# The order of small reductions on VectorE in a two-layer convolution kernel

## What is computed

```python
def _gn(v, G=8, eps=1e-5):
    g = v.reshape(B_, H_, W_, G, C_ // G)
    m = jnp.mean(g, axis=(1, 2, 4), keepdims=True)
    s = jnp.var(g, axis=(1, 2, 4), keepdims=True)
    return ((g - m) / jnp.sqrt(s + eps)).reshape(v.shape)

kern = jnp.einsum('lj,lk,li->ijkl', u, w, v)      # 3 x 3 x 16 x 16
y = lax.conv_general_dilated(_gn(x), kern, padding='SAME', ...)
x = x + jax.nn.relu(y + b)
```

## Time and profile before

| | |
|---|---|
| median of 3 runs | 5166.48 us (5156.98 to 5170.72) |
| profiled execution, device time | 5165.69 us |
| its span, first to last instruction | 5163.9 us |
| TensorE matmuls busy | 4731.3 us (92%) |
| VectorE busy | 2715.9 us (53%) |
| ScalarE busy | 2198.9 us (43%) |
| GpSimd busy | 1261.3 us (24%) |
| mean busy share of the DMA engines | about 0.3, 108 GB/s |
| chain of work that ended last | TensorE 88%, "issue" 9% |
| mean granted TensorE clock | 0.967 of full speed |

### The profile page before, as it was taken

One profiled execution on the slowest core, in us unless ns is written; L12 is line 12 of the kernel. 1 busy time (PEld: TensorE's weight loads), 2 busy tenths in 40 slices (PEclk: granted clock), 3 DMA queues, 4 the chain that ended last, 5 costly groups with the idle time before them and its releaser, 6 DMA issues.

```text
span 5163.9 us, 291702 instructions
## 1 busy us (share of the span) xinstructions
PE 4731.3 (92%) x139776; PEld 2677.6 (52%) x139776; DVE 2715.9 (53%) x3148; ACT 2198.9 (43%) x2242; POOL 1261.3 (24%) x1093
## 2 busy tenths in 40 slices
PE   6999999999999999999999999999999999999999
PEld 3555555555554555555555555555554555555555
DVE  4555555555555555555555555555555555555554
ACT  4343443444434434444344443443434434434343
POOL 3231222322212223122232231222312222222120
PEclk9999999999999999999999999999999999999999
DMA  3333333333333333333333333333333333333322
GB/s 113 102 108 109 105 113 106 112 109 106 113 106 105 113 106 109 109 110 109 106 112 109 110 108 109 102 116 104 110 105 110 111 104 112 109 102 117 103 84 97
DMA packets 542288, 555.89 MB, mean 108 GB/s; under 512 B 16432, under 2 KB 541104, under 8 KB 541104
## 3 DMA queue, kind: packets, MB, share of 16 engines
q1 hardware_dynamic: 541104, 537.22, 31.8%
HBM read 268.72 MB, written 268.44 MB: 104 GB/s over the span
## 4 chain that ended last, share of the span: by engine, by line
PE 88%; issue 9%; ACT 0%; DVE 0%; ACTq 0%; DVEq 0%
PE ps_y L379 35%; PE ps_y L337 26%; PE ps_x L404 11%; PE ps_x L359 9%; PE ps_y L341 4%; PE ps_y L311 2%; PE ps_x L292 1%; PE ps_x L302 0%; ACT relu L459 0%; PE ps_y L317 0%; ACT relu L462 0%; DVE result L564 0%; DVE pixels L579 0%; ACTq L457 0%; DVEq L95 0%
## 5 line engine op out<-in xcount | busy, mean ns | idle before, releaser
L379 PE MATMUL ps_y<-odds,scaled 32*32 32x512 f32 x49152 | 1876.0, 645 | 3.8 <-issue 0.5
L337 PE MATMUL ps_y<-evens,scaled 32*32 32x512 f32 x46080 | 1741.9, 598 | 11.6 <-issue 2.4
L379 PEld LDWEIGHTS ps_y<-odds,scaled 32*32 32x32 f32 x49152 | 879.0, 106 | 820.2 <-issue 414.8
L564 DVE TENSOR_TENSOR result<-ps_x,relu 128x2048 f32<-128x2048 f32 x256 | 586.7, 2292 | 1170.1 <-PE ps_x L404 920.7
L567 DVE TENSOR_TENSOR odds<-ps_x,relu 128x2048 f32<-128x2048 f32 x256 | 586.8, 2292 | 1125.7 <-PE ps_x L359 874.2
L462 ACT ACTIVATE relu<-ps_y,bias 128x2048 f32<-128x2048 f32 x256 | 503.7, 1968 | 1567.4 <-PE ps_y L379 1416.0
L337 PEld LDWEIGHTS ps_y<-evens,scaled 32*32 32x32 f32 x46080 | 816.7, 103 | 608.0 <-issue 185.5
L273 POOL TENSOR_TENSOR fold<-fold,evens 128x1024 f32<-128x1024 f32 x384 | 844.2, 2198 | 567.3 <-DVE evens L551 490.3
L459 ACT ACTIVATE relu<-ps_y,bias 128x2048 f32<-128x2048 f32 x256 | 503.6, 1967 | 932.4 <-PE ps_y L311 493.7
L404 PE MATMUL ps_x<-odds,constants 32*32 32x512 f32 x16384 | 776.7, 606 | 0.0
L359 PE MATMUL ps_x<-evens,constants 32*32 32x512 f32 x16384 | 767.9, 596 | 0.0
(11 more groups left out here) (46 smaller groups left out, 1513.3 us busy)
## 6 DMA issues: line engine op xcount, KB each, us to landing
out<-pixels SPq DMA_DIRECT2D x512, 512.0 KB, 3.5
raw<-in_x SPq DMA_DIRECT2D x256, 512.0 KB, 3.9
raw<-in_x SPq DMA_DIRECT2D x128, 576.0 KB, 4.2
raw<-in_x SPq DMA_DIRECT2D x128, 448.0 KB, 3.5
parameters<-in_params SPq DMA_DIRECT2D x2, 96.5 KB, 2.0
constants<-in_consts SPq DMA_DIRECT2D x1, 81.0 KB, 2.1
```

The costliest lines, as they stand in the source:

```text
L337: done = nc.tensor.matmul(ps_y[part, r, :], w0[rows, t * Q:(t + 1) * Q], N0[rows, k:k + EACH, i:i + HQ], start=(t == 0), stop=(t == NTAP - 1))
L379: done = nc.tensor.matmul(ps_y[Q * r:Q * (r + 1), q, :], w1[p % 2][Q * q:Q * (q + 1), t * Q:(t + 1) * Q], t1[Q * q:Q * (q + 1), k:k + EACH ...
L564: nc.vector.tensor_tensor(T2[:].rearrange("p q k h -> p q (k h)"), ps_x[:], R[:], ALU.add).then_inc(added, 1)
```

## The change

Two calls of `reduce_partials` move, each within its round of VectorE's layer-1 loop. In round 0, `reduce_partials(1, p)` goes from behind `turn_out` to behind `take_bias`, ahead of the add. In round 1, `reduce_partials(0, p + 1)` goes from behind `turn_out` to behind `variance(1, p)`, ahead of the add, of `scale_weights(1, p)` and of `turn_out`. Everything else, on VectorE and on the other engines, stays.

```diff
@@ -647,8 +647,12 @@
                 for f in range(ROUNDS):
                     if p and f == 0:
                         take_bias(1, p - 1)
+                    if p < IMAGES and f == ODDS_SUM - 1:
+                        reduce_partials(1, p)
                     if p < IMAGES and f == ODDS_SUM:
                         variance(1, p)
+                    if p + 1 < IMAGES and f == EVENS_SUM - 1:
+                        reduce_partials(0, p + 1)
                     if p + 1 < IMAGES and f == EVENS_SUM:
                         variance(0, p + 1)
                     if p:
@@ -659,10 +663,6 @@
                         scale_weights(0, p + 1)
                     if p:
                         turn_out(p - 1, f)
-                    if p < IMAGES and f == ODDS_SUM - 1:
-                        reduce_partials(1, p)
-                    if p + 1 < IMAGES and f == EVENS_SUM - 1:
-                        reduce_partials(0, p + 1)
```

## The result

The changed kernel takes 4696.21 us (median of 4 runs, 4694.12 to 4701.33), against 5164.54 us for the kernel before on the same chips. The ratio is 0.9095, with a 95% interval of 0.908 to 0.9111. The forecast was 4658 with a range of 4608 to 4725. So the direction was right, the stalls went as forecast, and the time lies in the range, 38 us above the forecast.

The account below looks back on a forecast made before the run. TensorE bounds the kernel: 348.0 us of idle stalls plus 159.4 of lowered clock, and about 1 us in p = 0, come off 5163.9, leaving a 4655.5 us span; forecast 4658 us, range 4608 to 4725.

Parts of the forecast that it names:

- What bounds the kernel: TensorE, at layer 1's group sums (L292): 348.0 us in 125 stalls, waiting for VectorE's reductions queued behind the transposes.
- The clock: TensorE's granted clock falls behind the stalls, mean 0.967; 159.4 us of the loss belong to the stalls.
- Part 1: VectorE, f = 0: reduce_partials(1), 0.53 us, goes behind take_bias, ahead of the add; costs nothing, sums ready 8 us early.
- The cover of 3.3 us: VectorE, f = 0: time between the moved reduction's end and the add's earliest start; without it 33 us cost.
- Part 2: VectorE, f = 1: reduce_partials(0), 1.24 us, goes behind variance(1), ahead of the add; 1.9 us of cover, cost nothing.
- Part 3, what is late next: TensorE's next possible waits: the add, 1.0 us early in both rounds, and mini_read, 1.0 us spare in f = 2.
- Part 4, the floor: TensorE's layer-1 round: 8.70 us plus 0.33 us of group-sum matmuls, so 9.0 us for f = 1 and f = 2.
- The check "from the other side": TensorE's round less its stall, 11.10 - 1.99 = 9.1 us, agreeing with the 9.0 us floor to 0.1 us.
- Rivals 3, 4 and 5: 3: half-clock stays, 4817, 0.03; 4: gapless TensorE granted less clock, 5166 and above, 0.02; 5: change does nothing, 5166, 0.01.
- Rival 2: Moved reductions stall VectorE ahead of the add, in f = 1 waiting for GpSimd's folds; slower than before; chance 0.01.
- Rival 1: In f = 2 mini_read or the add comes later than TensorE, a smaller wait: 4677 to 4720 us; chance 0.13.

Follow-up runs that it names:

- the three kernels that were chosen by it to be fast: Changed kernel with nine-matmul layer-0 group sums (4352 TensorE instructions an iteration) and 35, 27 or 57 matmuls more at the start: 4663.23, 4661.34, 4674.59 us.
- with 30 matmuls at the start: Changed kernel with nine-matmul layer-0 group sums (4352 TensorE instructions an iteration) and 30 small matmuls more at TensorE's start: 4786.28 us, ratio 0.9269.
- with 35: Changed kernel with nine-matmul layer-0 group sums (4352 TensorE instructions an iteration) and 35 small matmuls more at TensorE's start: 4663.23 us, ratio 0.9027.
- with 27: Changed kernel with nine-matmul layer-0 group sums (4352 TensorE instructions an iteration) and 27 small matmuls more at TensorE's start: 4661.34 us, ratio 0.9008.

## Why the prediction was right, and where its size was off

- **What bounds the kernel.** Right. Both stalls went with the reductions that were blamed for them, and each alone took its own stall away.
- **The clock.** Right for the change as a whole: no low stretch is left between the start and the end (0.997). Wrong would be to price a stall's share of it alone: the low clock followed 18 of the 63 short stalls in the kernel before, and 39 of them once the long stalls were gone; it followed all 62 long ones there, and 54 once the short ones were gone.
- **Part 1.** The cost of nothing was right, its working was not. The 0.53 us was read beside GpSimd's small copies; moved by 9 us, L599 stands beside the folds and takes 2 us. The cover of 3.3 us took it, and 1.50 us of it are left in the median. Moving an instruction had changed its duration, and the forecast did not look at what runs beside it in the new place.
- **Part 2.** Right, with a little more cover than worked out: 2.43 us of idle time is left in the median, and the run with five reductions more puts the onset at 3.6.
- **Part 3, what is late next.** Right: neither the add nor mini_read is waited for. TensorE's waits in the changed kernel name neither L404 nor, in layer 1, L292.
- **Part 4, the floor.** This is the step that failed, by its size. 9.0 us for f = 1 and f = 2 is right as the shortest round (8.99, and 8.95 but for one) and wrong as the mean (9.23 and 9.26): 0.23 x 63 + 0.26 x 62 = 31 of the 38 us. f = 3 has 0.10 x 64 = 6 us more. The check "from the other side" took one round of 11.10 us where the mean is 11.73; by the means f = 1 stood at 9.24 already in the kernel before, with its stall and its clock taken off, and f = 2 at 8.81, below the floor. The forecast's sum took all of the stall and the clock of f = 2 for gain, and 28 us of it didn't come. What holds the mean above the floor are the gaps at the block boundaries of TensorE's instructions: 68 us in the changed kernel, 46 in the kernel before, so 22 of the 38 us. That a part of them was hidden behind the 3.59 us stall of f = 2, because TensorE's queue could fill meanwhile, is argued; no run isolates it, and behind the 1.99 us stall of f = 1 nothing was hidden.
- **The rivals.** Rivals 3, 4 and 5 didn't happen. Rival 2 exists, 3.6 us away. Rival 1 in its form (a wait on mini_read or the add) didn't happen, though its time of 4677 to 4720 was near: the 4696 came from something that stood in none of the rivals.

## What to carry to other kernels

Where two engines wait for each other through a small step, put the step where its data is ready and its engine idle, and look first for what the bounding engine waits for, by matching times to within 0.1 us; here four moved lines of source gave 9% with no work saved. A stall of TensorE costs more than its length as long as the clock falls behind it, and how often it falls depends on the other stalls too. When the last stall of a fully unrolled TensorE stream is gone, its place in the blocks of 256 instructions is worth up to 2.6% in this kernel (4663 against 4786 us) and can be tried with a few dummy matmuls at the start. How long a gap is at a given place hangs on when the block is fetched, so a table of single rounds is a poor guide to the best place: the three kernels that were chosen by it to be fast missed their 4615 and 4630 us.

## What the runs showed of the hardware that was not expected

- TensorE's instructions come in packets of 16.4 KB, 256 instructions each (1095 packets for 280317 instructions). At a boundary the weight loads can stop, for up to 2.1 us with 30 matmuls at the start, until 1.2 to 1.6 us after a packet of the instruction queue has ended. It meets rounds with and without small matmuls (f = 3 of layer 1 with 30: 9.42 us in the mean against 8.68 with 35), and at other places a dense round doesn't show it (f = 3 of layer 0 with 27: 8.73 us in the mean, 8.74 at the longest). The Trainium skill (Runtime: NRT & Kernel Launch, "Instruction fetch mechanics") says that crossing such a boundary is mostly hidden. The traces agree by count, 74 gaps over 0.5 us at some 1090 crossings in the changed kernel, and show what the rest costs: 32 to 156 us of a run.
- A VectorE add of two one-element tensors in SBUF took 2.05 us in the median beside GpSimd's two-input add, and the same sum with one tensor and a per-partition scalar 0.214 us.
- A 2.0 us gap of TensorE was followed by the lower clock in 18 of 63 cases in one kernel and in 39 of 63 in another that differs only in a later gap. Gaps of 3.6 us were followed by it in all 62 cases of the first kernel, and in 54 of 62 where the 2.0 us gap is missing.
